# A decoder layer whose mixture-of-experts stage routes and scatters tokens group by group, into a memory region for each expert

## The reference

```
x = x + attention(layernorm(x))                      # 16 heads, one k and v for all
x = x + recurrent_attention(layernorm(x), ctx)       # 2 LSTM cells and attention over ctx, 64 steps in series
x = x + moe(layernorm(x))

def moe(x):                                          # 8 experts, 128 -> 512 -> 128
    logits = x @ router_W + router_b
    probs  = softmax(logits)
    top1   = argmax(probs)
    h      = relu(x @ W1[e] + b1[e])                 # for each expert e
    y      = h @ W2[e] + b2[e]
    return probs[top1] * y[top1]                     # only the chosen expert's result counts
```

## Time and profile before

| | us |
|---|---|
| median of 3 runs | 1859.98 |
| the profiled execution | 1860.22 |
| its span, first to last instruction | 1858.5 |
| loads, attention, second LayerNorm | 0 to 560.6 |
| recurrence | 560.6 to 1473.9 |
| third LayerNorm and routing | 1473.9 to 1562.1 |
| scatters | 1562.1 to 1644.5 |
| tiles | 1648.1 to 1849.6 |

### The profile page before, as it was taken

How to read it: one execution, slowest core, us unless ns; L and a number is a source line. 1 busy time by engine, 2 the same in 40 slices (tenths; PEclk the granted TensorE clock), 3 DMA queues, 4 the chain that set the end, 5 groups by cost and what they waited for, 6 DMA issues and landing times. The chain is left out here.

```text
span 1858.5 us, 82660 instructions
## 1 busy us (share of the span) xinstructions
PE 1480.6 (80%) x34335; PEld 1288.0 (69%) x34336; DVE 1148.7 (62%) x4397; ACT 730.6 (39%) x1849; POOL 221.5 (12%) x427
## 2 busy tenths in 40 slices
PE   1557777777756999999999999999999783049987
PEld 0446666666636888888888888888888672036665
DVE  5878888888883665665665666666666483024444
ACT  2445666656632443444444344344344210013332
POOL 0000000000001000000000000000000002743333
PEclk9768888889857999999999999999999755579999
DMA  6000000000035000000000000000000250222221
GB/s 215 1 2 0 0 0 0 0 0 0 1 91 208 0 0 0 0 0 0 0 0 0 0 0 0 0 0 0 0 0 0 66 173 34 104 76 71 72 72 49
DMA packets 42813, 57.39 MB, mean 31 GB/s; under 512 B 5754, under 2 KB 32892, under 8 KB 40856
## 3 DMA queue, kind: packets, MB, share of 16 engines
q1 hardware_dynamic: 36672, 42.90, 7.6%
q0 software_dynamic: 5376, 12.66, 1.9%
q10 hardware_dynamic: 728, 1.34, 0.2%
HBM read 30.52 MB, written 26.88 MB: 31 GB/s over the span
## 5 line engine op out<-in xcount | busy, mean ns | idle before, releaser
L1516 DVE TENSOR_TENSOR hb<-psH,b_sb 128x512 f32<-128x512 f32 x72 | 49.8, 691 | 169.0 <-issue 89.2
L900 PE MATMUL sc_a<-h_a,KH 128*128 128x48 f16 (+2 forms) x4096 | 123.9, 183 | 2.5 <-DVE h_a L1057 2.5
L900 PE MATMUL sc_b<-h_b,KH 128*128 128x48 f16 (+2 forms) x4096 | 122.9, 183 | 0.0
L860 PE MATMUL z_b<-h_b,WL 128*128 128x64 f16 x2304 | 112.3, 193 | 10.7 <-issue 2.4
L860 PE MATMUL z_a<-h_a,WL 128*128 128x64 f16 x2304 | 112.3, 194 | 9.5 <-DVE h_a L1049 1.8
L940 PEld LDWEIGHTS mx_a<-pmv_a,VH 128*128 128x128 f16 x4096 | 107.1, 96 | 16.6 <-DVE pmv_a L1085 16.2
L940 PEld LDWEIGHTS mx_b<-pmv_b,VH 128*128 128x128 f16 x4096 | 107.2, 96 | 16.0 <-DVE pmv_b L1085 16.0
L940 PE MATMUL mx_a<-pmv_a,VH 128*128 128x16 f16 x4096 | 113.1, 169 | 5.5 <-DVE pmv_a L1085 0.4
L940 PE MATMUL mx_b<-pmv_b,VH 128*128 128x16 f16 x4096 | 113.1, 169 | 5.1 <-DVE pmv_b L1085 0.4
L900 PEld LDWEIGHTS sc_a<-h_a,KH 128*128 128x128 f16 x4096 | 112.8, 96 | 2.6 <-DVE h_a L1057 2.6
L900 PEld LDWEIGHTS sc_b<-h_b,KH 128*128 128x128 f16 x4096 | 113.1, 96 | 0.0
(11 more groups left out here) (282 smaller groups left out, 3715.8 us busy)
## 6 DMA issues: line engine op xcount, KB each, us to landing
sorted_x<-zt SPq DMA_DIRECT2D x9, 1032.0 KB, 12.0
xr<-sorted_x SPq DMA_DIRECT2D x72, 65.0 KB
xg<-sorted_x SPq DMA_DIRECT2D x72, 64.0 KB
XT<-in_ctxT SPq DMA_DIRECT2D x1, 4096.0 KB, 13.1
x_scratch<-X SPq DMA_DIRECT2D x1, 4096.0 KB, 15.9
TOK<-x_scratch SPq DMA_DIRECT2D x4, 1024.0 KB, 10.4
w_sb<-in_w SPq DMA_DIRECT2D x1, 2048.0 KB, 12.8
b_sb<-in_b SPq DMA_DIRECT2D x1, 2048.0 KB, 19.4
```

Source lines behind the costliest of these rows:

```text
L860: mm = nc.tensor.matmul(q.z[layer][:, j * GB:(j + 1) * GB], WL[:, blk + j, w, :], mov[m], start=False, stop=False, skip_group_check=True)
L900: mm = nc.tensor.matmul(A.S[:, WIDE * n:WIDE * n + streamed(n)], KH[:, k, pair * P:(pair + 1) * P], A.h[1][:, 2 * n:2 * n + streamed(n) // ...
L1516: nc.vector.tensor_tensor(hb[:, u, :], psH[:, u, :], b1_sb[:, bass.ds(col, FF)], ALU.add).then_inc(v_hb, 1)
```

## The change

*Regions.* Each expert has its own region of `REGION` = 8192 + 128 rows in `sorted_x`, so the place of a token depends only on the tokens before it and not on the other experts' counts. Behind the eight regions are eight times 128 rows for tiles beyond the last token. A table `rtab` has the first row of each tile; SP reads it into a register for each load.

*Routing by group.* `choose` (which expert), `ranks` (the two count matmuls) and `place` (slots and gates) run for each group of 16 columns, with `base` carrying each expert's next row from group to group. POOL's scatters of a group wait for the slots and the gates of that group only. After the last group `tables` computes the tables.

*Presets.* The nine writes in the recurrence block and the fill of `zt` there are gone. In the last block POOL fills a `zt` of one row a partition, and SP writes it to the eight times 128 rows behind the regions, and, once the counts are known, to the 128 rows after each expert's last token.

*Tiles.* One load brings the whole rows into `xr`, now eight buffers (`RING`), and its wait is for the store of eight tiles before. `xg` is gone. `run_tiles` writes out the first 14 steps, then has 7 bodies of 8 steps, then the last 3.

*Order.* SP issues the loads of x1 before the router's. TensorE runs the last logits of a group before it turns back a later group.

```diff
+REGION = B * T + P
+NROWS = NE * REGION + NE * P
+RING = 8
-                    pool.memset(zt[:, :, :], 0.0).then_inc(v_zt, 1)
...
 SP, last block
+                        row = sync.value_load(rtab[0:1, bass.ds(j, 1)], min_val=0, max_val=NROWS - P)
+                        wait(sync, d_ys[u % 4], 4 * (j - u % 4) - 16)
+                        sync.dma_start(xr[:, u, :], xs_dram[bass.ds(row, P), :]).then_inc(d_x[u], 16)
+                    sync.wait_ge(v_zt, 2)
+                    for e in range(NE):
+                        sync.dma_start(xs_dram[NE * REGION + e * P:NE * REGION + (e + 1) * P, :], zt[:, :]).then_inc(d_z, 16)
+                    sync.wait_ge(v_last, 1)
+                    for e in range(NE):
+                        row = sync.value_load(lasti[0:1, e:e + 1], min_val=0, max_val=NROWS - P)
+                        sync.dma_start(xs_dram[bass.ds(row, P), :], zt[:, :]).then_inc(d_z, 16)
+                    sync.wait_ge(v_tab, 1)
+                    sync.wait_ge(d_z, 16 * 2 * NE)
                     sync.wait_ge(d_sc, 16 * T)
...
 POOL
-                    pool.wait_ge(v_sub, 3)
                     for t in range(T):
-                        pool.wait_ge(v_slot, 1)
+                        pool.wait_ge(v_slot, t // TG + 1)
+                        pool.wait_ge(v_gate, t // TG + 1)
                         pool.indirect_dma_start(xs_dram, bass.IndirectOffsetOnAxis(slot[:, t:t + 1], 0),
                                                 TOK[:, t, :], None).then_inc(d_sc, 16)
...
 TensorE
+                    for g in range(NG):
+                        group_logits(g)
+                        if g + 2 < NG:
+                            turn_back(g + 2)
+                        ranks(g)
...
 VectorE
+                    for g in range(NG):
+                        if g + 1 < NG:
+                            statistics(g + 1)
+                        if g + 2 < NG:
+                            add_a(g + 2)
+                        choose(g)
+                        if g + 1 < NG:
+                            normalise(g + 1)
+                        place(g)
+                    tables()
...
 run_tiles
+                head = RING + 6
+                for j in range(head):
+                    step(j, j % RING)
+                body = (NT - 2 - head) // RING * RING
+                with eng.Fori(head, head + body - RING + 1, RING) as j:
+                    for k in range(RING):
+                        step(j + k, (head + k) % RING)
```

More of the change, by code:

```diff
@@ L1133, in decoder_kernel @@
             xT = sb("xTc", [P, 2, 512])
[L1134 to L1140, removed]
+            lg = sb("lg", [P, TG, NE])
+            m1 = sb("m1", [P, TG])
+            eg = sb("eg", [P, TG, NE])
+            one = sb("one", [P, TG, NE])
+            tot = sb("tot", [P, NE, TG])
+            cum = sb("cum", [P, NE, TG])
+            keep = sb("keep", [P, NE, TG])
+            sl = sb("sl", [P, TG, NE])
+            first = sb("first", [P, NE])
+            base = sb("base", [P, NE])
             cnt = sb("cnt", [P, NE])
             cnti = sb("cnti", [P, NE], I32)
-            pad = sb("pad", [P, NE])
+            unit = sb("unit", [P, NE])
             end = sb("end", [P, NE])
@@ L1189, in decoder_kernel @@
             d_sc = sem("d_sc")
-            d_xg = [sem(f"d_xg{u}") for u in range(2)]
+            v_tab = sem("v_tab")
+            v_gate = sem("v_gate")
+            d_x = [sem(f"d_x{u}") for u in range(RING)]
             p_xt = sem("p_xt5")
@@ L1199, in decoder_kernel @@
             v_ys = sem("v_ys")
-            d_xr = [sem(f"d_xr{u}") for u in range(4)]
             v_yb = sem("v_yb")
@@ L1204, in decoder_kernel @@
             NCH = T // 4
-            x_rows = xs_dram.rearrange("(j p) d -> p j d", p=P)
             out_rows = out.rearrange("b t d -> (b t) d")
             def run_tiles(eng, step):
[L1211 to L1215, removed]
-                for j in range(NT - 2, NT + 1):
-                    step(j, j % 4)
+                head = RING + 6
[5 more added lines that the diff above has]
+                        step(j + k, (head + k) % RING)
+                for j in range(head + body, NT + 1):
+                    step(j, j % RING)
             def tile(j):
@@ L1300, in logits, with group_logits @@
                         for n in range(4):
[L1301 to L1303 removed]
+                            t = 4 * (c % CG) + n
+                            mm = nc.tensor.matmul(psH[:, c // CG % 2, t * NE:(t + 1) * NE], xT[:, c % 2, n * P:(n + 1) * P],
+                                                  rw_sb[:, :], start=True, stop=True)
                         mm.then_inc(p_l, 1)
[L1305 to L1309 removed]
+                    def group_logits(g):
                         for c in range(CG * g, CG * (g + 1)):
@@ L1431, in add_a, with step, statistics @@
                                                     ALU.add).then_inc(v_x2, 1)
-                    add_a(0)
-                    for g in range(NG):
+                    k = 0
+                    def step(ins):
+                        nonlocal k
+                        k += 1
+                        ins.then_inc(v_r, 1)
+                        dve.wait_ge(v_r, k)
+                    def statistics(g):
                         gs = slice(TG * g, TG * (g + 1))
@@ new lines, in _ @@
+                    add_a(0)
+                    statistics(0)
+                    add_a(1)
+                    normalise(0)
+                    dve.wait_ge(s_rw, 32)
+                    dve.wait_ge(v_c, 5 * NE + 2)
+                    for g in range(NG):
+                        if g + 1 < NG:
[6 more added lines that the diff above has]
+                        place(g)
```

242 lines of the change are left out of this document (117 added, 125 removed).

## The result

The changed kernel takes 1804.72 us (median of 4 runs, 1803.04 to 1806.68), the kernel before beside it 1859.38 (4 runs, 1858.69 to 1861.70): 0.9704 of the time, with a 95% interval of 0.9687 to 0.9721. The forecast was 1808.5, with a range of 1802 to 1822. The profiled execution has a span of 1803.2 us, 55.3 less than the 1858.5 of before; the forecast for that difference was 51.7. On another chip the same kernel took 21 us more, and its variants were as slow on two further ones; that is told with the experiments.

A forecast was written before the change was run, and what follows sets the result against it. Stages run in series, the scatter stage being one queue of 64 POOL scatters (81.43 us) after an 88.10 us wait; -44.6 + 0.3 - 1.9 + 0.7 - 7.0 + 0.8 = -51.7 us from 1860.22 gives 1808.5 us, range 1802 to 1822.

The forecast's parts named there:

- The first scatter: Routing: scatters start once the first group's gate stands, -44.6 us including 0.87 from x1's loads going first.
- POOL does not run dry: Scatter stage: each later group's gate comes before POOL asks, 3.4 us to spare for group 1; scatters keep 1.272 us each.
- The memset: Recurrence start: without POOL's fill of zt, the tiles TensorE waits for come earlier, -1.9 us.
- the nine writes: Recurrence: the writes of zt were beside it, so removing them gains 0.
- The load order: Third LayerNorm: SP issues x1's loads first, so VectorE's adds start earlier, -0.87 us.
- The router's data: Routing: router weights, now loaded behind x1, come 0 to 2 us late for TensorE; +0.3 us taken.
- SP's register read: SP's queue per tile: only the first read and load count, +0.7 us (0 to 1.2), 0.5 of it the read.
- the tiles: Tile stage: fourteen tiles written out and bodies of eight make it shorter, -7.0 us (bounds 0 and -11.3).
- Scatters beside a busy VectorE: Scatter stage: each of 64 scatters takes 0.012 us more beside VectorE's work, +0.8 us (at most +8.4).
- Rival 1: Scatter stage: XN and the scatters hold each other up, about +9 us, 1817.5 us in all; chance 0.20.
- rival 2: Tile stage gains nothing, because the pause at the loop's end grows with its body: 1815.5 us; chance 0.12.

The follow-up runs named there:

- e3: The changed kernel, but every scatter waits for the slots and gates of the last group: 1846.63 us, 0.9922 of the kernel before.
- e1: The changed kernel with the zt memset and its nine writes put back in the recurrence block: 1809.06 us, 0.9722 of the kernel before.
- e2: The changed kernel with only the zt memset put back in the recurrence block, without the writes: 1807.32 us, 0.9709 of the kernel before.
- e8: The changed kernel with the router's two loads ahead of x1's: 1825.56 us, 0.9800 of the kernel before.
- e10: The changed kernel with the router's two loads ahead of x1's, run again beside the unedited changed kernel: 1827.27 us, 0.9815 of the kernel before.
- e4: The changed kernel with all 73 steps of the tile stage written out, no loop: 1791.50 us, 0.9629 of the kernel before.
- e7: The changed kernel with 64 extra XN operations and 32 copies on VectorE behind the routing's tables: 1833.15 us, one run.

## Why the prediction was right, and where it was not

*The first scatter.* The bulk of the forecast, 43.7 us between the first add and the first scatter, came out at 44.0. The sum over the order of VectorE, step by step, with durations by size, was good to 0.3 us. e3 shows by itself that the start of the queue is worth 42 us, all but 2 of this term. The first scatter itself came at 1513.2, 3.4 us before the 1516.6 of the forecast. Only 0.3 of that is due to this part; the rest is the memset, the nine writes and the loads, told below.

*POOL does not run dry.* Forecast 3.4 us to spare before the seventeenth scatter; measured 4.0 (1530.05 to 1534.01), and 16.9 us from the first scatter to that gate, as worked out (1519.35 to 1536.3). With slow handoffs the claim is false: POOL waits 17 us for group 2, and the time, 1825.8, lies outside of the range. The prediction had no case for that, and no row of before could price it, since there nothing but POOL ran beside the scatters; that all engines might share something with the scatters, not just VectorE, was the missing rival.

*The memset* (-1.9, measured -2.2; TensorE's wait for POOL is 1.9 shorter, 6.99 to 5.08, and the other 0.3 is the moment at which the block began) and *the nine writes* (0, measured -2.1). Here the step "the nine writes of zt were beside the recurrence: 0" failed. They lay beside it and cost 2 us all the same, in one pause of all engines behind some 22 us of DMA at 414 GB/s; e1 and e2 tell the writes from the memset. This is most of the 3.6 us by which the sum was short.

*The load order* (-0.9, measured -1.6): beside the place in the queue, the first load of x1 also came 0.7 us sooner after its issue (6.22 us to the add, against 6.94). That is not the order's doing: in e8 and e10, with the router's loads first, it comes 6.42 and 6.21 us after its issue too. The order is worth the 0.9 of the forecast, and where the other 0.7 comes from stays open. The router's data were not waited for.

*SP's register read* (+0.7, measured +0.95; the read itself takes 0.27) and *the tiles* (-7.0, measured -6.7) came as worked out, the last by its own rows: 2.61 and 3.23 us. e4 confirms both parts of the loop's price and rules out that code fetched anew costs it.

*Scatters beside a busy VectorE* (+0.8, measured +0.3). Four scatters around XN of group 2 took 0.98 to 1.08 in place of 0.97, those beside XN of group 3 took 0.97, and XN took the same 4.19 both times. What lengthens the few is not shown. e7 repeats it with 64 XN operations. The rule of the Trainium skill (SBUF — State Buffer, "Who interferes with whom") that such an operation and GpSimd's descriptor writing exclude one another for a whole instruction is not borne out for these forms here, if it is taken for the whole 0.97 us of a scatter: by it e7's row would have been much longer than 16.54 us, or its scatters longer than 1.01. How much of a scatter's time is descriptor writing, and in which mode XN ran, no row shows.

*Chances.* Rival 1 had 0.20 and rival 2 0.12; both are refuted, the first by the scatters beside XN here and in e7, the second by the bodies of 21.48 us. The lateness of gates that rival 1 priced at 5 us does occur, by another mechanism, and costs 17.

## What to carry to other kernels

Where a queue of fixed pace (here 64 scatters of 1.27 us) stands idle until a whole is computed, what cutting the work into groups gains is the earlier start of the first, no more, and it can be read from the order of the engine that computes; then look how little slack each later group has, since any slowness of the small steps comes out there. A transfer that is "beside" other work is not free when it fills the DMA engines: leave it out, or make it small. Measure an overlapped stage on more than one chip before trusting a gain of 2%, and write a short loop out when its end costs 0.6 us and each step 0.16 more.

## What the runs showed of the hardware that was not expected

- Some way into a run of scatters (8 to 18 us), in the sets on three of the chips, many instructions of VectorE and SP start 0.70 us apart or a multiple, and ACT and TensorE stand up to 25 us; elsewhere the same code has its steps of 0.32 us and less. The cause is open.
- Nine writes of 1 MB at 414 GB/s are followed by one pause of 1.3 (e1) or 2.4 us (before) in a recurrence that touches none of their data; without them it is gone, and some 2 us with it.
- A POOL scatter of 128 rows (0.97 us) and a float32 `tensor_scalar` of 128x128 on VectorE (0.26 us) run beside one another at full pace: 12 scatters and 64 such operations in e7.
- 72 tiles of written-out code, each run once, start every 2.45 us without a pause; the same in a loop of eight takes 2.61 and 0.62 more at its end.
